# A fused block on one core: short instructions for three weight preparations, smaller last gather groups, and an attention prologue whose weights are loaded first

## What is computed

```python
x = x + _L0_conv_ref(_ln_c(x), ...)      # local attention: 8 heads, each token sees 7 neighbours of 64
t = t + _L0_ffn_ref(_ln_t(t), ...)       # mixture of experts, GELU: 2 shared, 8 routed, top 2
x = x + _L1_conv_ref(_ln_c(x), ...)      # attention within windows of 64 tokens, with bias and mask
t = t + _L1_ffn_ref(_ln_t(t), ...)       # mixture of 8 spline experts (KAN), top 2
```

## Time and profile before

| | us |
|---|---|
| median of 3 runs | 947.11 |
| lowest and highest | 940.69, 947.17 |
| the profiled execution, as timed | 947.09 |
| its span, first to last instruction | 945.2 |

### The profile page before, as it was taken

How to read it: one execution, slowest core, us unless ns; L and a number is a source line. 1 busy time by engine, 2 the same in 40 slices (tenths; PEclk the granted TensorE clock), 3 DMA queues, 4 the chain that set the end, 5 groups by cost and what they waited for, 6 DMA issues and landing times.

```text
span 945.2 us, 21806 instructions
## 1 busy us (share of the span) xinstructions
PE 789.3 (84%) x7434; PEld 739.1 (78%) x7434; DVE 611.0 (65%) x1256; ACT 559.2 (59%) x1339; POOL 295.7 (31%) x320
## 2 busy tenths in 40 slices
PE   4987999778930089546999999999999999999992
PEld 3865677777920078446999999999999999999992
DVE  3888987704006359655477777777777777777752
ACT  4862422454620179233677787777777777777650
POOL 1760012534348348301212222223232322222111
PEclk9995999898975569555999999999999999999997
DMA  9602967576779100117054554315453633420000
GB/s 342 266 3 81 381 251 292 215 262 235 217 266 397 40 2 3 49 48 310 10 203 154 177 167 150 111 39 183 119 200 111 211 111 111 161 61 9 9 7 6
DMA packets 51297, 141.07 MB, mean 149 GB/s; under 512 B 6202, under 2 KB 29124, under 8 KB 46116
## 3 DMA queue, kind: packets, MB, share of 16 engines
q1 hardware_dynamic: 40116, 114.00, 32.9%
q0 software_dynamic: 9136, 9.77, 5.5%
q10 hardware_dynamic: 1984, 16.52, 4.4%
HBM read 106.65 MB, written 33.62 MB: 148 GB/s over the span
## 4 chain that ended last, share of the span: by engine, by line
PE 51%; DVE 3%; ACT 1%; DMA 1%; issue 1%; POOL 0%; DVEq 0%; POOLq 0%; ACTq 0%
PE kan_ps_h L1543 32%; PE kan_ps_y L1557 16%; PE kan_ps_slots L1224 1%; PE kan_ps_slots L1232 1%; DMA kan_slot_x<-normed_dram,slots 1%; PE kan_ps_lists L1210 1%; PE kan_ps_x L1531 0%; PE kan_ps_h L1206 0%; DMA out<-kan_y_sb,kan_slots_y 0%; ACT kan_xt L1590 0%; DVE kan_hf L1692 0%; DVE kan_hfar L1688 0%; DVE kan_hnear L1689 0%; ACT kan_hnear L1604 0%; DVE kan_hf L1696 0%
## 5 line engine op out<-in xcount | busy, mean ns | idle before, releaser
L1543 PE MATMUL kan_ps_h<-kan_xf,kan_w 128*128 128x128 f32 x2496 | 306.0, 276 | 0.0
L1543 PEld LDWEIGHTS kan_ps_h<-kan_xf,kan_w 128*128 128x128 f32 x2496 | 292.9, 193 | 0.0
L1557 PE MATMUL kan_ps_y<-kan_w,kan_hf 128*128 128x128 f32 x1248 | 154.1, 277 | 8.3 <-DVE kan_hf L1696 8.3
L1557 PEld LDWEIGHTS kan_ps_y<-kan_w,kan_hf 128*128 128x128 f32 x1248 | 147.3, 194 | 8.8 <-issue 8.8
L1773 POOL DMA_INDIRECT out<-kan_y_sb,kan_slots_y x39 | 63.3, 1624 | 237.8 <-ACT kan_y_sb L1641 237.8
L1688 DVE TENSOR_TENSOR kan_hfar<-kan_ht,kan_hfar 128x1024 f32<-128x1024 f32 x39 | 47.9, 1229 | 84.4 <-ACT kan_hnear L1604 84.4
L540 DVE TENSOR_TENSOR sw_raw<-sw_raw,sw_scal 128x4096 f32<-128x4096 f32 x8 | 35.4, 4425 | 89.2 <-DMA sw_scal<-in_scalers 89.2
L958 POOL DMA_INDIRECT f_slot_x<-normed_dram,f_tokens x39 | 49.4, 1265 | 135.9 <-DVE f_rows L1074 67.7
L1590 ACT ACTIVATE kan_ht<-kan_hu,kan_biases 128x256 f32<-128x256 f32 x156 | 66.2, 496 | 13.6 <-DVE kan_hu L1715 13.6
L256 PE MATMUL a_ps_Z<-consts,a_xn 128*128 128x128 f32 x32 | 10.7, 334 | 74.5 <-ACT a_xn L329 74.5
L928 ACT ACTIVATE f_slot_h<-f_ps_up,f_wr 128x128 f32<-128x128 f32 x156 | 44.7, 371 | 36.2 <-DMA f_wr<-in_experts 20.6
(11 more groups left out here) (243 smaller groups left out, 1626.8 us busy)
## 6 DMA issues: line engine op xcount, KB each, us to landing
kan_w<-w_dram SPq DMA_DIRECT2D x16, 2048.0 KB, 7.7
kan_w<-w_dram SPq DMA_DIRECT2D x16, 1024.0 KB, 5.2
sw_raw<-in_experts SPq DMA_DIRECT2D x6, 2048.0 KB, 10.2
w_dram<-sw_raw SPq DMA_DIRECT2D x5, 2048.0 KB, 11.9
sw_raw<-in_experts SPq DMA_DIRECT2D x6, 1024.0 KB, 11.9
w_dram<-sw_raw ACTq DMA_DIRECT2D x3, 2048.0 KB, 8.0
f_wr<-in_experts SPq DMA_DIRECT2D x20, 258.0 KB, 4.7
w_dram<-sw_raw SPq DMA_DIRECT2D x5, 1024.0 KB, 14.7
```

Of the source, the lines that this page charges most:

```text
L1543: mm = eng.matmul(ps_h[n % 2][:, m, :], w12[n % 2][:, at:at + P], rhs, start=(c == 0), stop=(c == BASES))
L1557: mm = eng.matmul(ps_y[n % 2][:, :], lhs, w3[n % 2][:, i * P:(i + 1) * P], start=(i == 0), stop=(i == CH1 * FEAT - 1))
```

## The change

Three edits.

**Preparation in pieces.** For the experts 5, 6 and 7 `prepare` is replaced by the new `prepare_in_pieces`, which does the same products and differences in instructions of 512 columns. **Smaller last groups.** The gathers back are grouped by `BACKS` = 0, 8, 16, 24, 28, 30, 32 in place of four groups of eight; each group has a semaphore of its own. **Attention's prologue.** ScalarE waits for the weights only ahead of the second turn of its loop, VectorE makes `shift` right behind the statistics, and in `load1` the transfers are issued ahead of the clearing of semaphores. The first two touch the block of the GELU experts only; the third touches both attentions, `load1` only the second.

```diff
--- before.py
+++ after.py
@@ -319,9 +319,8 @@
             @block.scalar
             def _(eng):
                 stats_scalar(eng)
-                arrived(eng)
                 eng.preload_act_table(ACT.Exp)
-                eng.wait_ge(ready, 2)
+                eng.wait_ge(ready, 1)
 
                 @stage
                 def norm(n):
@@ -382,6 +381,9 @@
                     eng.activation(probsT[n % 2][:, :, :], ps_P[:, :, :], ACT.Copy).then_inc(probsT_ok, 1)
 
                 for i in range(TILES + LAST):
+                    if i == 1:
+                        arrived(eng)
+                        eng.wait_ge(ready, 2)
                     copy_probs(i - 8)
                     copy_k(i - 3)
                     copy_x(i - 2)
@@ -427,14 +429,14 @@
             @block.vector
             def _(eng):
                 stats_vector(eng)
+                eng.scalar_tensor_tensor(shift[:, :], moments[:, :, 0], -1.0, rstd[:, :], ALU.mult, ALU.mult)\
+                   .then_inc(ready, 1)
                 arrived(eng)
                 fill(eng, logits)
                 half = consts[:, C_HALF:C_HALF + 2]
                 if bq is not None:
                     eng.tensor_scalar(q_bias[:, :], half, bq, DK ** -0.5, ALU.mult, ALU.mult)
                 eng.tensor_scalar(q_scale[:, :], half, DK ** -0.5, None, ALU.mult).then_inc(ready, 1)
-                eng.scalar_tensor_tensor(shift[:, :], moments[:, :, 0], -1.0, rstd[:, :], ALU.mult, ALU.mult)\
-                   .then_inc(ready, 1)
 
                 @stage
                 def add_bias(n):
@@ -532,6 +534,28 @@
     def prepare(self, eng, e):
         self.begin(eng, e)
         self.finish(eng, e)
+
+    def prepare_in_pieces(self, eng, e):
+
+        a = e % self.BUFFERS
+        first, scal12, last, scal3 = self.views(e)
+        eng.wait_ge(self.loaded[a], 48 * (e // self.BUFFERS + 1))
+        for c in range(BASES):
+            ins = eng.tensor_tensor(first[:, c, :], first[:, c, :], scal12, ALU.mult)
+        ins.then_inc(self.scaled[a], 1)
+        for k in range(CH1):
+            for c in (slice(0, FOLDS), slice(FOLDS, BASES)):
+                ins = eng.tensor_tensor(last[:, k, c, :], last[:, k, c, :],
+                                        scal3[:, k, :].unsqueeze(1).to_broadcast([P, FOLDS, P]), ALU.mult)
+        ins.then_inc(self.scaled[a], 1)
+        eng.wait_ge(self.scaled[a], 2 * (e // self.BUFFERS) + 1)
+        for c in range(FOLDS):
+            ins = eng.tensor_tensor(first[:, c, :], first[:, c, :], first[:, FOLDS + c, :], ALU.subtract)
+        ins.then_inc(self.folded[a], 1)
+        eng.wait_ge(self.scaled[a], 2 * (e // self.BUFFERS) + 2)
+        for k in range(CH1):
+            eng.tensor_tensor(last[:, k, 0:FOLDS, :], last[:, k, 0:FOLDS, :], last[:, k, FOLDS:, :],
+                              ALU.subtract).then_inc(self.folded[a], 1)
 
     def begin(self, eng, e):
         a = e % self.BUFFERS
@@ -648,7 +672,7 @@
         wr = [sb(f"wr{i}", [P, ROW0]) for i in range(W_BUFFERS)]
         begun = wr[0][:, 0:SLOT_TILES * EXPERTS].rearrange("p (n e) -> p n e", e=EXPERTS)
         back = [wr[m // (ROW0 // P)][:, m % (ROW0 // P) * P:(m % (ROW0 // P) + 1) * P] for m in range(PAIRED)]
-        BACK = 8
+        BACKS = [0, 8, 16, 24, 28, 30, PAIRED]
         slot_h = [sb(f"slot_h{i}", [P, CH0, P]) for i in range(2)]
         slot_y = [sb(f"slot_y{i}", [P, P]) for i in range(Y_BUFFERS)]
 
@@ -689,7 +713,7 @@
         in_x = [sem(f"in_x{i}") for i in range(X_BUFFERS)]
         in_up = [sem(f"in_up{i}") for i in range(W_BUFFERS)]
         in_down = [sem(f"in_down{i}") for i in range(W_BUFFERS)]
-        in_back = [sem(f"in_back{i}") for i in range(PAIRED // BACK)]
+        in_back = [sem(f"in_back{i}") for i in range(len(BACKS) - 1)]
         out_y = [sem(f"out_y{i}") for i in range(Y_BUFFERS)]
         x_turned = sem("x_turned")
         x_copied = sem("x_copied")
@@ -959,11 +983,11 @@
                                                in_offset=bass.IndirectOffsetOnAxis(ap=tokens[:, n:n + 1], axis=0))\
                            .then_inc(in_x[n % X_BUFFERS], 16)
 
-                def gather_back(m):
+                def gather_back(m, j):
                     t, k = divmod(m, CHOICES)
                     eng.indirect_dma_start(out=back[m], out_offset=None, in_=routed_dram,
                                            in_offset=bass.IndirectOffsetOnAxis(ap=rows[:, k, t:t + 1], axis=0))\
-                       .then_inc(in_back[m // BACK], 16)
+                       .then_inc(in_back[j], 16)
 
                 eng.wait_ge(kept, 32)
                 eng.wait_ge(tokens_ok, 1)
@@ -973,8 +997,9 @@
                 eng.wait_ge(y_summed, SLOT_TILES)
                 for b in range(Y_BUFFERS):
                     eng.wait_ge(out_y[b], 16 * len(range(b, SLOT_TILES, Y_BUFFERS)))
-                for m in range(PAIRED):
-                    gather_back(m)
+                for j in range(len(BACKS) - 1):
+                    for m in range(BACKS[j], BACKS[j + 1]):
+                        gather_back(m, j)
 
             @block.vector
             def _(eng):
@@ -1089,13 +1114,13 @@
                 splines.finish(eng, 4)
 
                 for e in range(5, EXPERTS):
-                    splines.prepare(eng, e)
+                    splines.prepare_in_pieces(eng, e)
 
                 eng.wait_ge(added, STEPS)
 
                 def add_routed(j):
-                    eng.wait_ge(in_back[j], 16 * BACK)
-                    for m in range(j * BACK, (j + 1) * BACK):
+                    eng.wait_ge(in_back[j], 16 * (BACKS[j + 1] - BACKS[j]))
+                    for m in range(BACKS[j], BACKS[j + 1]):
                         t, k = divmod(m, CHOICES)
                         if k >= 1:
                             eng.wait_ge(measured, m)
@@ -1103,15 +1128,15 @@
                         eng.scalar_tensor_tensor(xt, back[m], weight[:, k, t:t + 1], xt, ALU.mult, ALU.add)\
                            .then_inc(measured, 1)
 
-                def measure(g):
-                    eng.wait_ge(measured, CHOICES * GROUP * (g + 1))
-                    for t in range(g * GROUP, (g + 1) * GROUP):
+                def measure(j):
+                    eng.wait_ge(measured, BACKS[j + 1])
+                    for t in range(BACKS[j] // CHOICES, BACKS[j + 1] // CHOICES):
                         ins = eng.bn_stats(stats[:, t, :], x_sb[:, t, :])
                     return ins
 
-                for g in range(TURNS):
-                    add_routed(g)
-                    ins = measure(g)
+                for j in range(len(BACKS) - 1):
+                    add_routed(j)
+                    ins = measure(j)
                 chain.after(ins)
 
 
@@ -1900,11 +1925,11 @@
             s_w1 = sem("s_w1")
 
             def load1(eng):
-                for s in gelu_sems:
-                    eng.sem_clear(s)
                 eng.dma_start(w1_sb[:, :], d["w1"]).then_inc(s_w1, 16)
                 eng.dma_start(bp_row[:, :], d["rows1"][:, P:]).then_inc(s_w1, 16)
                 eng.dma_start(bv_col[:, :], d["rows1"][0:1, 0:P].rearrange("o p -> p o")).then_inc(s_w1, 16)
+                for s in gelu_sems:
+                    eng.sem_clear(s)
                 splines.all_stored(eng)
 
             def arrived1(eng):
```

## The result

| | before | after |
|---|---|---|
| median, us | 944.58 | 934.30 |
| lowest and highest of 4 runs | 940.69, 947.17 | 933.01, 936.47 |
| the profiled execution, as timed | 947.09 | 936.47 |
| its span | 945.2 | 934.6 |

What follows compares the result with a forecast made beforehand. Blocks run serially, so time lost handing over from the first expert layer to the second attention (268 to 331 us, TensorE idle) is lost whole. Gains 4.3+2.5+4.4=11.2 us, from 947.1, forecast 935.9 us; range 929.5 to 940.5.

Steps and rivals of the forecast that it cites:

- Short instructions, 4.3: Gathers back beside expert 7's preparation: 512-column instructions let them through at boundaries, so POOL's last gather ends 4.3 us earlier.
- the rival by which pieces do nothing: Gathers back: splitting VectorE's instructions gains nothing, POOL still ends at 316.6, total gain 6.9, 940.2 us; chance 0.05.
- every second gather then loses about 0.55: Beside expert 7's pieces: alternate gathers come 0.05 late and wait 0.55; some seven lose 1.8 us instead of 6.1.
- none does: Gathers back beside expert 7's pieces: if no gather misses a boundary, POOL's gain is 6.1 us.
- Smaller last groups, 2.5: End of the gathers back: two additions and one statistic, 1.05 us, behind the last landing instead of 3.6; gain 2.5.
- The floor of 315.0: End of the gathers back: VectorE's backlog would keep the stage's end at about 315 even were POOL held by nothing.
- a VectorE with no wait at its last group: End of the gathers back: VectorE waiting for no landing at its last group would show the forecast wrong.
- Prologue, 4.4: Start of the second attention: earlier weight transfers and table load bring TensorE's first transpose to 326.35 from 330.78; bounds 3.4 to 4.5.
- ScalarE waiting for weights ahead of its second normalisation: Attention's prologue: such a wait would show the forecast wrong; it was reckoned to cost 0.
- before or with the table's end: Second attention's prologue: the last weights land at 325.7, when the Exp table load ends, so waiting for them costs 0.
- First attention, 0: Prologue of the first attention: no wait for weights to remove, gain 0 us, cost 0.1 at most; normalisation still about 11.1.
- Experts 5 and 6, 0: Slot stage: these preparations' later end and shorter gather stalls are hidden, so 0 us; at most 2.8 was available.

## Where the prediction held and where it failed

The gain was right to 1 us (11.2 against 10.3 by the medians), and that closeness is in part luck: two of its terms were wrong in opposite directions. What was put as 4.3+2.5+4.4=11.2 is 6.0+0+4.1 in the profiles, and another 0.6 of their difference was chance.

- **Short instructions, 4.3: the mechanism right, the size not.** Boundaries do let gathers through, pieces of 1024 columns lose the gain, and the rival by which pieces do nothing fell. The failed step is "every second gather then loses about 0.55". It took the pace of 0.60 us a piece from the window bias, which is right alone, but left out that a gather holds VectorE back in turn: with gathers beside them two pieces take 1.25. None of the following gathers missed a boundary, and the term was 5.98. The bound given for "none does", 6.1, was the right value; over all profiles the term is 4.7 to 6.0, above 4.3 in each. The step rested on a difference of 0.05 us between two periods, measured where they did not run side by side.
- **Smaller last groups, 2.5: wrong, 0.** The failed step is that the eight additions and four statistics behind the last landing set the stage's end. The rows showed 0.99 us between VectorE's last statistic (321.79) and the attention's first row (322.78), which the prediction left unexplained. In kernels where VectorE really ends the block it is 0.60. POOL's own row, a memset with 6.42 us of idle time put down to its sequencer, stood in the trace of before and was not read. The prediction named what is queued on VectorE, and never asked what POOL does between its last gather and the block's end. That is the 5.88 us of the drain. With the drain gone the groups are worth 1.3 to 1.9.
- **The floor of 315.0** by VectorE's backlog: the third group landed at 306.31, not 307.5, and VectorE was done at 313.65. In after this is hidden, since POOL reaches the end only at about 316. The picture of a VectorE with no wait at its last group, which the prediction named as a sign that it is wrong, did come: the backlog is real, only its cost is not seen.
- **Prologue, 4.4: right, 4.1.** The first transpose came 3.62 us after the attention's first row, in the predicted 3.6 to 4.6. The named sign of being wrong, ScalarE waiting for weights ahead of its second normalisation, did come, for 0.55 us. That the weights arrive "before or with the table's end" was 0.66 us too early: the last transfer took 2.77 from issue to use (2.28 in the row of before), VectorE used it at 319.77, and the table load ended at 319.11. From the first transpose to the first product it took 1.08 in place of 0.82, so the wait cost 0.3.
- **First attention, 0:** the normalisation starts at 11.34 in place of 11.10, with the row ahead of it later by as much.
- **Experts 5 and 6, 0:** held, by the kernel with expert 7 alone in pieces.
- **The clock** was no term: 0.98 in the spline stage of both, and 498.3 us in both.

What stays open: why the slot stage ends anywhere from 264 to 272 and the second attention takes 62.0 to 64.6, the largest parts of what the profiled executions differ by; how far each edit of the prologue carries its 4.1; and why the prologue alone moved the whole time by 2.2 where its profile shows 4.05, though the interval holds both.

## What to carry to other kernels

When two engines finish near a block's end, read the first row of each engine in the next block and the idle time in its brackets, and shorten the one whose end plus its own closing time is last; the gap behind the engine that you mean to shorten tells whether it is the one (here 0.60 if it is, 0.92 or more if it is not). Where a long instruction with two SBUF operands stands beside indirect DMAs of POOL, cut it into pieces that are short against a gather's period (0.60 to 1.25 worked, 1.14 to 1.25 did not), and only where POOL is on the path. Before you leave a drain out, look where it comes back: at the end of the next block, or nowhere if the program ends.

## What the runs showed of the hardware

The end of a block costs time on POOL where it has issued indirect DMAs: the drain is over 5.88 us behind POOL's last gather in each of the nine profiles that have it, against 0.07 us behind POOL's last instruction at the end of the attention, where it issues none. Behind the landing of the last scatter, at the end of the program, it takes 6.42 us. Left out, it is paid at the end of the next block (5.88 there in place of 0.07), where it may be hidden. Leaving it out in both blocks brought 6.9 us beside after on the same chip (933.67 to 926.73).

A gather beside a long VectorE instruction with two operands in SBUF is held (5.13 and 2.21 us); beside a reduction of 4.42 us with one it is not (0.94). It passes at the first boundary although the next instruction stands right behind, ending 0.90 or 0.91 us after it, and it holds VectorE back by some 0.05 us in turn (two pieces in 1.25 us in place of 1.20).
